# Scan stages of a state-space and feed-forward kernel: the place of the raw copy, the owner of one product, the order of the row and column copies, and the waits of the down projection

## The chip, the cores and the metric

The kernel runs on one core of a Trainium2 chip. The core has TensorE (PE), VectorE (DVE), ScalarE (ACT) and GpSimd (POOL), and a SyncE (SP) queue that issues most of the copies between memory and SBUF. The metric is the device time of one execution in microseconds (us); lower is better.

## The reference, cut to what matters

The input `x` is (4, 1024, 1024) in float32. First a selective state-space layer (Mamba) with `x`'s layer norm as its gate:

```
x  = in_proj_w @ ctx                       # 1024 channels, 1024 time steps, 4 sequences
u  = silu(causal_conv4(x) + conv_b)
x_dbl = x_proj_w @ u                       # rows: 32 of dt, 16 of B, 16 of C
delta = softplus(dt_proj_w @ dt + dt_b)
state[n] = state[n] * exp(delta * A[n]) + delta * u * B[n, t]      # n = 0..15, scan over t
y = sum_n state[n] * C[n, t] + D * u
out = x0 + tanh(g0) * y * silu(layernorm(x0))
```

Then a layer that picks 128 of the 1024 rows of each sequence by a score, runs rotary attention and a gated feed-forward (`silu(h @ w_gate) * (h @ w_up) @ w_down`, width 4096) on the 512 picked rows together, and writes them back into `x` scaled by a gate.

## The kernel before, in words

The four sequences are worked on two at a time. The order of stages is: `project_stage` (input projection, convolution and `x_dbl` for sequences 0 and 1), `scan_stage(0)`, `route_stage(0)` and `layer_stage(0)` (choice, attention), `scan_stage(2)`, `route_stage(2)` and `layer_stage(2)`.

**A scan stage** has `UNITS` = 32 units. A unit is 128 channels (`e` = 0..7) by 512 time steps (one half `th` of a sequence); eight units are a chunk `c`, so that chunks 0 and 2 are the first halves of the two sequences (called even below) and chunks 1 and 3 the second ones (odd). A unit holds 16 states in `NPAIR` = 8 pairs, and every engine walks through slots 0 to 7 of it:

- ACT makes `exp(delta * A)` for both states of pair `i` in slot `i` (L1214), before which `release` (L1103 to L1114) waits until pair `i-2` has left the PSUM banks; beside these it carries the unit's other copies, each tied to a slot by a constant (`READ_AT`, `COPY_AT`, `DU_COPY_AT`, and `RAW_AT`, `PRE_AT`).
- `B * delta * u` comes from POOL for pairs 0, 2, 4, 6 (L733) and from PE for pairs 1, 3, 5, 7 (`make_b`, L862 and L864).
- DVE scans state after state (L1290). The product with C is done by POOL (L757, from the three SBUF buffers `hp`) for the pairs that `pool_pairs` names, and by DVE (L1267, from PSUM) for the others. PE adds the products up (`add_pair`, L882), DVE gates the sum (L1256), POOL adds `x` (L765), SP stores.
- In odd chunks each scan starts from `carry`, saved in the even one.

**The rows of B and C** of a chunk are copied to all 128 partitions by SP: `load_B(c, g)` with 0.5 to 1 MB and `load_C(c, g)` with 1 MB for each group `g` of four states, each after a wait that the chunk before has used the old rows. The B columns (`load_columns`, tile `k_BT`, L129) are eight copies of 2 KB a chunk, double buffered; POOL makes diagonals of them in the chunk's last unit (L747) and ACT scales with them (L1092). SP's list is written out by hand and strictly in order; its first entry of unit `s` is `load_u(s + 2)`, which waits until PE has done `skip(s)` (L869) in slot 3.

**Beside the scans**, `scan_stage(0)` (`early`) projects and convolves sequences 2 and 3: PE runs `late_projection(s)` in slots 1 to 3 of unit `s` and `late_convolution(s - 1)` in slots 5 to 7; ACT's `copy_raw` moves the projection out of PSUM (L1184, L1188, L1191), `copy_pre` the convolution. `scan_stage(2)` (`fill`) runs the feed-forward of the rows picked from sequences 0 and 1 in the gaps of PE: output projection, then `gate_up` in slots from unit 6 to unit 26, then `down` for half of the columns from slot 6 of unit 26. Its weights go through a ring of four tiles that SP fills (L644). POOL's `merge` (L773) multiplies up and gate parts into `hidden`, two of the 32 blocks at a time, and counts `hidden_ready`; `down(m, a)` reads block `m`.

Of the kernel before, what the change touches and what calls it, by code (L numbers as in the profile page):

```python
# [25 lines left out]
NE = DI // P  # L26
NK = DC // P
NS, NR, TAPS = 16, 32, 4
# [3 lines left out]
H2 = L // HALF  # L32
# [4 lines left out]
NI = 4096 // P  # L37
RMS_EPS = 1e-6
SPAN = 2
# [51 lines left out]
class Kept:  # L91
# [22 lines left out]

    def load_delta(self, sp, t, b, sem):
        sp.dma_start(self.dt[:, 0], t["xd"][b * ND:b * ND + NR, 0:HALF]).then_inc(sem, 16)
        self.load_columns(sp, t, b, 0, 0, sem)

    def load_states(self, sp, t, b, g, sem):
        at = b * ND + NR + 4 * g  # L120
# [2 lines left out]
        at += NS  # L123
        sp.dma_start(self.bC[:, 4 * g:4 * g + 4], t["xd"][at:at + 4, 0:HALF].partition_broadcast(P)).then_inc(sem, 16)

    def load_columns(self, sp, t, b, th, j, sem):
        for k in range(NS // 2):
            at = b * ND + NR + 4 * (k // 2) + 2 + k % 2
            sp.dma_start(self.BT[:, j, k], t["xd"][at:at + 1, th * HALF:(th + 1) * HALF].rearrange("n (a p) -> p (n a)", p=P),  # L129
                         allow_slow_non_contiguous=True).then_inc(sem, 16)  # L130
# [238 lines left out]


def pool_pairs(first, s):
    return (1, 3, 5, 6, 7) if s // NE % H2 else (1, 3, 5, 7)


def vec_pairs(first, s):
# [30 lines left out]
FILL_END = DOWN_FROM + DOWN_HALF  # L406
SIZE_LAG, LOG_LAG, SIGMOID_LAG, SWISH_LAG, UP_LAG, MERGE_LAG = 3, 3, 6, 5, 3, 4
WEIGHTS_AT = (0, 2, 5)
RAW_AT, PRE_AT = 0, 3
LATE_PROJECTION = ((), (0, 1), (2,), (3,), (), (), (), ())  # L410
LATE_CONVOLUTION = ((), (), (), (), (), (0,), (1,), (2, 3))

# [1 line left out]
def scan_stage(nc, t, ctx, keep, first, late_taps=None):  # L414
# [93 lines left out]
    def chunk(s):  # L508
        return s // NE
# [42 lines left out]
    with nc.Block() as block:  # L552
        @block.sync
        def _(sp):
# [28 lines left out]
            def load_dt(c):  # L583
                b, th = first + c // H2, c % H2
                if c >= 2:
                    sp.wait_ge(dt_done, NE * (c - 1))
                sp.dma_start(dt[:, c % 2], xd[b * ND:b * ND + NR, th * HALF:(th + 1) * HALF]).then_inc(dt_in[c % 2], 16)
                if c >= 2:
                    sp.wait_ge(xT_ready, NT * NE * (c - 1))
                    if scaled:  # L590
                        sp.wait_ge(diag_ready, ND_B * (c - 1))
                keep.load_columns(sp, t, b, th, c % 2, BT_in[c % 2])

            def load_B(c, g):
                if c >= SPAN * H2:
# [64 lines left out]
                sp.dma_start(ln2[:], t["cols"][:, NH + 2 * NKV + KT:]).then_inc(ln2_in, 16)  # L660
            for s in range(UNITS):
                c, e = chunk(s) + 1, s % NE
                load_u(s + 2)
                load_end(s + 1)
                if e == 0 and s:
                    load_C(c - 1, 2)
                    load_C(c - 1, 3)
                if e == 0 and c < SPAN * H2:
                    load_dt(c)
                if fill:  # L670
                    for k in weights_at(s, 0):
                        load_weights(k)
                if e == NE - 1:
                    load_B(c, 0)
                    load_B(c, 1)
                if fill:
                    for k in weights_at(s, 1):
                        load_weights(k)
                if e == NE - 1:
                    load_B(c, 2)  # L680
                    load_C(c, 0)
                if early and s + 1 < UNITS:
                    load_late(s + 1)
                    if e == 2 and c < SPAN * H2:
                        load_ctx(c)
                if early and s >= 2:
                    store_pre(s - 2)
                if e == NE - 1:
                    load_B(c, 3)
                    load_C(c, 1)  # L690
                if s:
                    store(s - 1)
                if fill and s == (WO_DONE[1] + BASE_LAG) // NPAIR:
                    sp.wait_ge(base_ready, H2 * SPAN)
                    sp.dma_start(t["base0"].rearrange("(a p) c -> p a c", p=P), base).then_inc(base_out, 16)
                if fill:
                    for k in weights_at(s, 2):
                        load_weights(k)
            store(UNITS - 1)
            if early:  # L700
                store_pre(UNITS - 2)
# [117 lines left out]
        def _(pe):  # L819
# [109 lines left out]
            def down(m, a):  # L929
                tile = TILES_UP + m // 2  # L930
                if m % 2 == 0 and a == 0:
                    pe.wait_ge(w_in[tile % RING], 16 * (tile // RING) + 16)
                if m == 0:
                    pe.wait_ge(swish_ready, NI // 2)
                    pe.wait_ge(up_ready, NI // 2)
                    pe.wait_ge(hidden_ready, NI // 2)
                last = nc.tensor.matmul((p_gate, p_up)[a][:], hidden[:, m, a * P:(a + 1) * P],
                                        ring[:, tile % RING, m % 2 * HALF:(m % 2 + 1) * HALF], start=m == 0, stop=m == NI - 1)
                if m % 2 == 1 and a == 1:
                    last.then_inc(w_used, 1)  # L940
# [102 lines left out]
        def _(act):  # L1043
# [162 lines left out]
            for s in range(UNITS):  # L1206
                act.wait_ge(delta_ready, s + 1)
                for i in range(NPAIR):
# [13 lines left out]
                    if s + 1 < UNITS:  # L1222
# [3 lines left out]
                            softplus_exp(s + 1)  # L1226
                        elif i == READ_AT + 2:
                            softplus_ln(s + 1)
                    if early and i == RAW_AT and s:
                        if s == 1:  # L1230
                            act.wait_ge(halo_made, 1)
                        copy_raw(s - 1)
                    if early and i == PRE_AT and s >= 2:
                        copy_pre(s - 2)
                    if i == COPY_AT:
# [5 lines left out]
                    if i > DU_COPY_AT:  # L1241
                        make_states(s + 1, PARTS_AT[i - 1] % PARTS, PARTS_AT[i])
            if early:
                copy_raw(UNITS - 1)
                copy_pre(UNITS - 2)
                copy_pre(UNITS - 1)
            if fill:
# [1149 lines left out]
```

## Time and profile before

| what | value |
|---|---|
| median of 3 runs | 2808.98 us (2807.94 to 2814.0) |
| the profiled execution | 2810.57 us, of which its span 2808.7 us |
| PE, PE weight loads | 2534.9 us (90%), 1853.5 us (66%) |
| DVE | 1964.8 us (70%) |
| ACT, POOL | 1616.4 us (58%), 1616.2 us (58%) |
| first scan of the first stage to the last one's end | 160 to 955 us |
| the same of the second scan stage | 1248 to 2106 us |

Busy shares are means over stages with different limits. A row of the timeline gives start, duration, engine, line, operation, tiles written and read, the count of instructions merged in it, and in brackets how long the engine had stood idle and what it waited for. Durations of neighbours on an engine overlap a little, so the pace is read from start to start.

### The profile page before, as it was taken

What the parts mean: (1) busy time and instruction counts of PE and PEld (TensorE: products, weight loads), DVE (VectorE), ACT (ScalarE), POOL (GpSimd) and SP (SyncE); (2) the same over time, 40 slices, a digit from 0 to 9 for tenths busy, and PEclk for the clock granted to TensorE, in tenths of its full rate; (3) what the DMA queues carried; (4) which work ended last, traced back from release to release, by engine and by line L of the source; (5) the groups of instructions that cost most, each with busy time, mean ns of one, the idle gap of its engine ahead of it and who ended that gap; (6) DMA issues with size and microseconds to landing.
All of it is one profiled execution on the core that took longest, in us unless ns stands there. A gap on an engine that the chain in (4) does not pass through costs nothing. (4 is left out here: it accounts for less than half of the span.)

```text
span 2808.7 us, 38267 instructions
## 1 busy us (share of the span) xinstructions
PE 2534.9 (90%) x13528; PEld 1853.5 (66%) x13528; DVE 1964.8 (70%) x2500; ACT 1616.4 (58%) x3482; POOL 1616.2 (58%) x898
## 2 busy tenths in 40 slices
PE   8979999989999657879999999999997799999998
PEld 3356666666666426556688988888673576578853
DVE  5679999989999786569998988999896544110000
ACT  4578888778887442277787787887661215210000
POOL 1269999999999610028899998889881100000000
PEclk9979999999999858999999999999998899999999
DMA  7732242442332397863344344244228741344442
GB/s 277 260 87 83 64 144 80 127 115 64 116 92 80 110 405 263 291 192 99 121 135 129 103 153 146 84 167 146 85 76 311 273 151 38 97 158 150 152 155 97
DMA packets 252622, 412.53 MB, mean 147 GB/s; under 512 B 50832, under 2 KB 134800, under 8 KB 249872
## 3 DMA queue, kind: packets, MB, share of 16 engines
q1 hardware_dynamic: 238928, 353.98, 39.4%
q10 hardware_dynamic: 12160, 51.39, 4.6%
q0 software_dynamic: 1344, 4.72, 0.5%
q8 instruction: 108, 1.77, 0.3%
q14 instruction: 82, 0.67, 0.1%
HBM read 325.09 MB, written 84.94 MB: 146 GB/s over the span
## 5 line engine op out<-in xcount | busy, mean ns | idle before, releaser
L757 POOL TENSOR_TENSOR s_x<-s_hp,k_bC 128x1024 f32<-128x1024 f32 x288 | 680.2, 2368 | 68.2 <-DVE s_hp L1290 67.7
L733 POOL TENSOR_TENSOR s_x<-s_du,k_bB 128x1024 f32<-128x1024 f32 x254 | 601.5, 2377 | 39.2 <-PE s_py L882 23.6
L882 PE MATMUL s_py<-k_ident,s_x 128*128 128x128 f32 x4096 | 522.2, 274 | 21.4 <-POOL s_x L757 21.4
L882 PEld LDWEIGHTS s_py<-k_ident,s_x 128*128 128x128 f32 x4096 | 463.8, 142 | 32.6 <-POOL s_x L757 28.5
L1214 ACT ACTIVATE s_pA<-s_delta,k_negA 128x512 f32<-128x512 f32 x512 | 333.6, 681 | 190.6 <-DVE s_x L1267 185.1
L1983 PE MATMUL l_p<-l_hT,l_ring 128*128 128x256 f32 x1792 | 389.4, 380 | 2.0 <-ACT l_hT L2088 1.0
L1983 PEld LDWEIGHTS l_p<-l_hT,l_ring 128*128 128x128 f32 x1792 | 341.6, 191 | 49.6 <-issue 1.5
L1290 DVE TENSOR_TENSOR_SCAN s_hp<-s_x,s_carry,s_pA 128x512 f32<-128x512 f32 x256 | 321.7, 1267 | 44.5 <-PE s_pA L864 36.1
L1214 ACT ACTIVATE s_x<-s_delta,k_negA 128x512 f32<-128x512 f32 x512 | 340.6, 710 | 0.0
L1290 DVE TENSOR_TENSOR_SCAN s_hp<-s_x,s_pA 128x512 f32<-128x512 f32 x256 | 310.0, 1211 | 42.3 <-ACT s_x L1214 26.5
L1092 ACT ACTIVATE s_xT<-s_duT,k_BT 128x128 f32<-128x128 f32 x1024 | 336.4, 389 | 0.1
L864 PEld LDWEIGHTS s_pA<-k_bB,s_duT 128*128 128x128 f32 x2048 | 251.0, 196 | 86.2 <-DVE s_hp L1290 68.0
L1290 DVE TENSOR_TENSOR_SCAN s_pA<-s_pA,s_x 128x512 f32<-128x512 f32 x256 | 299.8, 1214 | 4.4 <-ACT s_pA L1214 4.0
L864 PE MATMUL s_pA<-k_bB,s_duT 128*128 128x128 f32 x2048 | 262.8, 283 | 23.0 <-DVE s_hp L1290 23.0
L1267 DVE TENSOR_TENSOR s_x<-s_pA,k_bC 128x1024 f32<-128x1024 f32 x224 | 268.7, 1199 | 17.7 <-DMA k_bC<-scratch_xd 17.7
L1290 DVE TENSOR_TENSOR_SCAN s_pA<-s_pA,s_carry,s_x 128x512 f32<-128x512 f32 x192 | 234.6, 1268 | 1.0 <-ACT s_pA L1214 0.8
L1960 POOL DMA_INDIRECT out_dram<-c_rows,l_row_i x2 | 1.9, 953 | 330.8 <-DVE c_rows L2309 330.8
L862 PEld LDWEIGHTS s_pA<-k_ident,s_xT 128*128 128x128 f32 x1024 | 116.5, 142 | 97.4 <-DVE s_hp L1290 72.1
L862 PE MATMUL s_pA<-k_ident,s_xT 128*128 128x128 f32 x1024 | 135.9, 276 | 39.1 <-DVE s_hp L1290 39.1
L2304 DVE TENSOR_TENSOR t_hidden<-l_silu,l_p 128x256 f32<-128x256 f32 x32 | 13.5, 421 | 208.0 <-PE l_p L1983 208.0
L1990 PE MATMUL l_p<-l_ring,t_hidden 128*128 128x512 f32 x352 | 151.4, 592 | 0.0
L1950 POOL TENSOR_TENSOR l_squares<-l_squares,l_minus_half 128x1 f32<-128x1 f32 x2 | 1.1, 555 | 250.3 <-DVE l_squares L2280 250.3
(238 smaller groups left out, 3770.4 us busy)
## 6 DMA issues: line engine op xcount, KB each, us to landing
k_bC<-scratch_xd SPq DMA_DIRECT2D x32, 1024.0 KB, 11.0
scratch_ug<-p_ug ACTq DMA_DIRECT2D x16, 1024.0 KB, 4.1
k_u<-scratch_ug SPq DMA_DIRECT2D x64, 256.0 KB, 3.5
k_bB<-scratch_xd SPq DMA_DIRECT2D x32, 512.0 KB, 8.3
s_gy<-scratch_ug SPq DMA_DIRECT2D x64, 256.0 KB, 4.5
s_xt<-in_x SPq DMA_DIRECT2D x64, 256.0 KB, 4.8
scratch_x<-s_xt SPq DMA_DIRECT2D x64, 256.0 KB, 3.6
r_x<-scratch_x SPq DMA_DIRECT2D x32, 512.0 KB, 10.2
```

Of the source, the lines that this page charges most:

```text
L733: pool.tensor_tensor(out=x[:, 4 * g:4 * g + n], in0=du[:, s % 2:s % 2 + 1].broadcast_to([P, n, HALF]), in1=bB[:, into:into + n], op=ALU.mu ...
L757: pool.tensor_tensor(out=x[:, 2 * i:2 * i + 2], in0=hp_of(s, i), in1=bC[:, 2 * i:2 * i + 2], op=ALU.mult).then_inc(pool_hc, 1)
L862: last = nc.tensor.transpose(out, xT[:, k, a * P:(a + 1) * P], ident[:])
L864: last = nc.tensor.matmul(out, duT[:, a * P:(a + 1) * P], diagB[:, 2 * scaled.index(i) + n % 2, a], start=True, stop=True)
L882: last = nc.tensor.matmul(py[:, a], x[:, n, a * P:(a + 1) * P], ident[:], is_transpose=True, start=False, stop=n == NS - 1 and a == HALF / ...
L1092: last = nc.scalar.activation(xT[:, k, a * P:(a + 1) * P], duT[:, a * P:(a + 1) * P], ACT.Copy, scale=BT[:, chunk(s) % 2, column(2 * TURNE ...
L1214: nc.scalar.activation(out, delta[:, s % 2], ACT.Exp, scale=negA[:, s % NE, n:n + 1]).then_inc(dA_ready, 1)
L1267: nc.vector.tensor_tensor(x[:, 2 * i:2 * i + 2], pA[:, j:j + 2], bC[:, 2 * i:2 * i + 2], ALU.mult).then_inc(vec_hc, 1)
L1290: nc.vector.tensor_tensor_scan(out, dA, added, initial, ALU.mult, ALU.add).then_inc(scanned, 1)
L1983: last = nc.tensor.matmul(out[:, 0:ROWS], w[:, c * P:(c + 1) * P], src[:, c], start=c == 0, stop=c == KT - 1)
L1990: last = nc.tensor.matmul(banks[2 * a + h][:], src[:, a * P:(a + 1) * P], w[:, h * HALF:(h + 1) * HALF], start=is_first, stop=is_last)
L2304: nc.vector.tensor_tensor(hidden[:, m], silu[:, m % 2], acc[2 + m % 2][:, 0:ROWS], ALU.mult).then_inc(act_ready, 1)
```

## The change

1. `copy_raw(s)` is done in slot 6 of unit `s` and no longer in slot 0 of unit `s + 1`.
2. `pool_pairs` is (1, 3, 5, 7) in every chunk; in odd chunks it was (1, 3, 5, 6, 7). DVE multiplies pair 6 there.
3. `load_C(c, 2)` is asked for at the end of a chunk's last unit and `load_C(c, 3)` as the first entry of the next unit; both stood behind `load_u` and `load_end` of that unit.
4. The eight column copies, in one row in a chunk's first unit, become two at the end of each of its first four units.
5. `down` waits at its first block for all but the last merge, and for the last at block 28.

```diff
-        self.load_columns(sp, t, b, 0, 0, sem)
+        self.load_columns(sp, t, b, 0, 0, range(NS // 2), sem)
...
-    def load_columns(self, sp, t, b, th, j, sem):
-        for k in range(NS // 2):
+    def load_columns(self, sp, t, b, th, j, which, sem):
+        for k in which:
...
 def pool_pairs(first, s):
-    return (1, 3, 5, 6, 7) if s // NE % H2 else (1, 3, 5, 7)
+    return (1, 3, 5, 7)
...
-RAW_AT, PRE_AT = 0, 3
+RAW_AT, PRE_AT = 6, 3
...
                 sp.dma_start(dt[:, c % 2], xd[b * ND:b * ND + NR, th * HALF:(th + 1) * HALF]).then_inc(dt_in[c % 2], 16)
+
+            def load_columns(c, which):
+                b, th = first + c // H2, c % H2
                 if c >= 2:
                     sp.wait_ge(xT_ready, NT * NE * (c - 1))
                     if scaled:
                         sp.wait_ge(diag_ready, ND_B * (c - 1))
-                keep.load_columns(sp, t, b, th, c % 2, BT_in[c % 2])
+                keep.load_columns(sp, t, b, th, c % 2, which, BT_in[c % 2])
...
             for s in range(UNITS):
                 c, e = chunk(s) + 1, s % NE
+                if e == 0 and s:
+                    load_C(c - 1, 3)
                 load_u(s + 2)
                 load_end(s + 1)
-                if e == 0 and s:
-                    load_C(c - 1, 2)
-                    load_C(c - 1, 3)
...
                     for k in weights_at(s, 2):
                         load_weights(k)
+                if e < NS // 4 and c < SPAN * H2:
+                    load_columns(c, (2 * e, 2 * e + 1))
+                if e == NE - 1:
+                    load_C(c, 2)
...
                     pe.wait_ge(up_ready, NI // 2)
+                    pe.wait_ge(hidden_ready, NI // 2 - 2)
+                if m == NI - 4:
                     pe.wait_ge(hidden_ready, NI // 2)
...
-                    if early and i == RAW_AT and s:
-                        if s == 1:
+                    if early and i == RAW_AT:
+                        if s == 0:
                             act.wait_ge(halo_made, 1)
-                        copy_raw(s - 1)
+                        copy_raw(s)
...
             if early:
-                copy_raw(UNITS - 1)
                 copy_pre(UNITS - 2)
```

## Rows read from the trace of the kernel before

**Rows 1.** Timeline of DVE, unit 3 of the first scan stage.

```profile
235.72 2.35 DVE L1290 TENSOR_TENSOR_SCAN s_pA<-s_pA,s_x 128x512 f32<-128x512 f32 x2
239.26 1.22 DVE L1290 TENSOR_TENSOR_SCAN s_hp<-s_x,s_pA 128x512 f32<-128x512 f32 x1 [1.20 <-ACT s_x L1214]
...
256.88 1.20 DVE L1290 TENSOR_TENSOR_SCAN s_hp<-s_x,s_pA 128x512 f32<-128x512 f32 x1
...
260.28 2.34 DVE L1290 TENSOR_TENSOR_SCAN s_pA<-s_pA,s_x 128x512 f32<-128x512 f32 x2
```

**Rows 2.** Timeline of ACT in the same unit.

```profile
236.78 0.58 ACT L1184 ACTIVATE s_raw<-s_p_in 128x512 f32<-128x512 f32 x1
...
237.54 0.97 ACT L1092 ACTIVATE s_xT<-s_duT,k_BT 128x128 f32<-128x128 f32 x3
...
238.51 1.32 ACT L1214 ACTIVATE s_x<-s_delta,k_negA 128x512 f32<-128x512 f32 x2
...
255.65 1.32 ACT L1214 ACTIVATE s_x<-s_delta,k_negA 128x512 f32<-128x512 f32 x2
```

**Rows 3.** Timeline of DVE, unit 13 of the first scan stage (an odd chunk).

```profile
481.25 2.44 DVE L1290 TENSOR_TENSOR_SCAN s_pA<-s_pA,s_carry,s_x 128x512 f32<-128x512 f32 x2
484.79 1.28 DVE L1290 TENSOR_TENSOR_SCAN s_hp<-s_x,s_carry,s_pA 128x512 f32<-128x512 f32 x1 [1.10 <-PE s_pA L864]
...
491.35 0.69 DVE L1256 TENSOR_TENSOR s_gy<-s_py,s_gy 128x512 f32<-128x512 f32 x1 [0.62 <-PE s_py L882]
...
505.97 1.26 DVE L1290 TENSOR_TENSOR_SCAN s_pA<-s_pA,s_carry,s_x 128x512 f32<-128x512 f32 x1
```

**Rows 4.** Window in that chunk: length, busy us of PE, PEld, DVE, ACT, POOL, PE clock, DMA.

```profile
456.00:530.00 74.00, 68.43 (x427) 49.52 (x426) 68.84 (x61) 59.30 (x127) 73.76 (x37) 1.00 0.23 65
```

**Rows 5.** Timeline of DVE, unit 9, the second of that odd chunk.

```profile
385.32 2.44 DVE L1290 TENSOR_TENSOR_SCAN s_pA<-s_pA,s_carry,s_x 128x512 f32<-128x512 f32 x2
...
401.43 1.20 DVE L1267 TENSOR_TENSOR s_x<-s_pA,k_bC 128x1024 f32<-128x1024 f32 x1
402.55 1.27 DVE L1290 TENSOR_TENSOR_SCAN s_hp<-s_x,s_carry,s_pA 128x512 f32<-128x512 f32 x1
...
408.43 1.27 DVE L1290 TENSOR_TENSOR_SCAN s_pA<-s_pA,s_carry,s_x 128x512 f32<-128x512 f32 x1
```

**Rows 6.** Waits of the whole span: us in total, times, longest.

```profile
DVE s_x L1267 <- DMA k_bC<-scratch_xd: 17.7, 6, 3.7
```

**Rows 7.** Groups by line and shape, 160 to 955 us: busy us, mean ns, idle before.

```profile
L1267 DVE TENSOR_TENSOR s_x<-s_pA,k_bC 128x1024 f32<-128x1024 f32 x112 | 134.3, 1199 | 8.1 <-DMA k_bC<-scratch_xd 8.1
```

**Rows 8.** Timeline of DVE, unit 16 of the first scan stage.

```profile
567.83 0.69 DVE L1256 TENSOR_TENSOR s_gy<-s_py,s_gy 128x512 f32<-128x512 f32 x1 [2.01 <-PE s_py L882]
```

**Rows 9.** Timeline of SP's queue, unit 8 of the second scan stage.

```profile
1469.81 1.00 SPq L613 DMA_DIRECT2D k_bC<-scratch_xd  x2
...
1471.55 10.84 SPq L129 DMA_DIRECT2D k_BT<-scratch_xd  x8
1482.43 0.50 SPq L644 DMA_DIRECT2D s_ring<-in_w_up  x1
```

**Rows 10.** Timeline of PE, second scan stage, units 9 and 26.

```profile
1486.83 2.93 PE L924 MATMUL s_p_up<-s_h2T,s_ring 128*128 128x256 f32 x6 [3.09 <-DMA s_ring<-in_w_up]
...
1972.60 1.60 PE L937 MATMUL s_p_gate<-s_ring,t_hidden 128*128 128x512 f32 x2 [4.10 <-POOL t_hidden L773]
```

**Rows 11.** Timeline of ACT, unit 26 (the last copy of an up part).

```profile
1966.56 0.58 ACT L1134 ACTIVATE t_hidden<-s_p_up 128x512 f32<-128x512 f32 x1
```

**Rows 12.** Windows in the second scan stage, columns as in rows 4.

```profile
1484.90:1491.80 6.90, 4.97 (x17) 4.41 (x18) 2.21 (x3) 3.95 (x9) 5.56 (x3) 0.51 0.66 239
1700.00:1703.40 3.40, 3.40 (x17) 3.35 (x16) 3.40 (x4) 3.40 (x10) 3.40 (x2) 0.50 0.43 15
1973.10:1979.90 6.80, 6.80 (x9) 2.21 (x8) 0.51 (x1) 2.41 (x4) 6.26 (x3) 0.50 0.00 0
...
1542.00:1672.00 130.00, 129.83 (x889) 117.00 (x888) 119.56 (x108) 102.70 (x213) 125.09 (x64) 1.00 0.35 115
```

## The prediction

> **What bounds the kernel now.** I read the page first, for which stages each engine is busy in, then only the two scan stages, since nothing else is touched. In them three views answer: windows (who is full), the timeline of each engine over one unit (where DVE stands idle, for DVE carries the scans and sets the pace), and SP's timeline at a chunk's edge. A unit's length is the time between its first scan and the next unit's.
>
> Even units of the first scan stage last 24.56 us (235.72 to 260.28) and hold one idle time of DVE, 1.20 us at pair 1, which waits for ACT's exponential [rows 1]. ACT comes late to it because of the raw copy: from its first instruction to the one behind it ACT spends 237.54 - 236.78 = 0.76 us, and the exponential follows at 238.51 [rows 2]. Thirteen such units look alike, 2 to 7 and 17 to 23.
>
> Odd units there last 24.72 us, and DVE stands idle 1.10 + 0.62 us in each, both times for PE [rows 3], which is itself held up by POOL's products: POOL is busy 73.76 of 74 us [rows 4]. POOL is the bound of odd chunks. What DVE could do is seen in the chunk's second unit, before POOL has fallen behind: 23.11 us (385.32 to 408.43) [rows 5].
>
> At each chunk's edge DVE waits for the C rows of group 2: six waits, 17.7 us in all [rows 6], of which 8.1 in the first scan stage [rows 7], so 9.6 in the second. In unit 16 DVE waits another 2.01 us for the sum of the unit before [rows 8], again POOL's arrears.
>
> The second scan stage is PE's: 129.83 of 130 us busy, though POOL with 125.09 and DVE with 119.56 are close [rows 12]. There PE stands still twice for something this change moves: 3.09 us for a weight tile that SP asked for late, and 4.10 us at the first block of the down projection for POOL's last merge [rows 10]. After each the granted clock is half, 1.2 GHz, for 6.9 and 6.8 us, and once more for 3.4 us just after the edge at unit 16 [rows 12].
>
> **The change part by part.**
>
> *Raw copy to slot 6.* The 0.76 us of ACT leave the front of pair 1. The wait there falls from 1.20 to 1.20 - 0.76 = 0.44 us. They come back ahead of pair 7, whose exponentials began at 255.65 [rows 2]; the first takes half of the merged 1.32, so it ended near 256.34, and DVE took pair 7 up at 256.88 [rows 1]. That is some 0.5 us of cover, so 0.76 - 0.5 = 0.26 us comes out as a new wait. Net 0.76 - 0.26 = 0.5 us a unit, for units 1 to 7, 16 and 17 to 23: 15 x 0.5 = 7.5. Bounds: the whole 0.76 is won (11.4), or the new wait is as long as the old one was (0). The copy needs the projection, which PE ends in slot 3, and late convolution reads it a unit later, so nobody else is made to wait. In odd units DVE isn't waiting for ACT now, and the copy is shorter by the halo's; I take nothing.
>
> *Pair 6 to DVE, first scan stage.* A product costs DVE 402.55 - 401.43 = 1.12 us of its pace [rows 5]. An odd unit at DVE's own pace becomes 23.11 + 1.12 = 24.2; with POOL no longer full I take 24.1, as its wait of some 0.2 at pair 1 shrinks when the raw copy leaves. Units 11 to 15 and 27 to 31, ten of them, gain 24.72 - 24.1 = 0.6 each: 6.0. Two behind each edge lose, since they run at the 23.1 of unit 9 today: 4 x 1.0 = 4.0. Units 8 and 24 take the 1.12 too and get, as I choose, half of it back from a POOL that has less to catch up with: 1.0 lost together. Where an odd chunk ends, unit 16's 2.01 goes [rows 8]. Sum: 6.0 - 4.0 - 1.0 + 2.0 = 3.0. Bounds: nothing at all hidden, 16 x 1.12 = 17.9 lost against those 2.0; or 24.72 comes down to 23.7, which makes 7.
>
> *C rows earlier.* The request of group 2 moves from behind `load_u`, which stands until slot 3, to the end of the unit before, nearly half a unit sooner. DVE's waits are at most 3.7 us long [rows 6] and end with this copy. What is late next would be group 3, which moves forward too, or group 1, asked for where it was. I take all 8.1 in the first stage. In the second PE is the bound, and DVE's wait costs only what PE can't work through; I take two thirds of the 9.6, 6.4. Bounds: 0 if another copy takes its place, and all 9.6 with half of the 3.4 us at half clock, 11.3.
>
> *Columns in pairs.* Eight copies hold SP for 10.84 us, and the weight tile of `w_up` is asked for only behind them, at 1482.43 [rows 9]; PE then waits till 1486.83 [rows 10]. Without them and without the two C requests (1469.81 to 1471.55) the tile is asked for 1482.43 - 1469.81 = 12.6 us earlier and the wait goes: 3.09. At half clock 4.97 us of PE work were done that full clock does in half: 2.5. Together 5.6; bounds 3.09 and 3.09 + 3.45. Two copies at the end of four units stand ahead of `load_u`, which waits anyway; cost nothing, and if that cover were gone up to 10.84 / 4 = 2.7 us of SP a unit.
>
> *Down in two steps.* PE waits 4.10 us for the merge. The other conditions of the first block were met: the last up part was copied by 1966.56 + 0.58 = 1967.14 [rows 11], 5.5 us before PE went on at 1972.60. Block 28 comes five units later (26 entries of PE's list a unit, 4 a block), so the second wait costs nothing. With the clock: 4.10, and PE was busy all of the 6.8 us, so up to half of them, 3.4. PE's idle time was also a chance for DVE and POOL to catch up, so I take a little less than the 7.5, 6.5; bounds 4.1 and 7.5.
>
> *Pair 6 to DVE, second scan stage.* 16 odd units get 1.12 us more of DVE and 2.33 less of POOL. In the window of some five such units DVE is free 130 - 119.56 = 10.4 us, 2.1 a unit, more than the 1.12 [rows 12]. I take 0. Bounds: 16 x 1.12 = 17.9 lost; or 0.3 a unit, 5, won since POOL too was nearly full.
>
> Sum: 7.5 + 3.0 + 8.1 + 6.4 + 5.6 + 6.5 = 37.1. The profiled execution's own time is 2810.57, 1.9 more than its span, so 2773.5; it stood 1.6 above the median of the runs, 2808.98, which gives 2772, the time I predict.
>
> **The rivals.**
>
> *A, PE keeps its time in the second stage.* The C rows and the weights come sooner, but PE meets the next limit at once, or DVE's extra product eats what it gives: 6.4 + 5.6 = 12 lost from the sum, 2784. For it: PE is full there. Against: the half clock and the waits are PE's own.
>
> *B, the wait for C rows only moves.* The request comes sooner, but right behind 0.5 MB and 1 MB copies of the same edge; DVE then waits for group 1 or 2 as long. 8.1 + 6.4 = 14.5 lost, 2786.5. Against: behind the last request of the old unit SP asks for nothing until slot 3, so the engines of the copies have that time.
>
> *C, slower: the product joins the chain.* With pair 6 in PSUM, ACT may not begin the next unit's pair 0 until DVE has multiplied (`release`), and the scan waits for that exponential: product 1.12 and exponential 0.7 us in line, 1.8 a unit in 32 odd units, 58 us, in place of my 3.0: 2772 + 3 + 58 = 2833. It decides from (37.1 - 3.0) / 32 = 1.07 us a unit on, so the product alone, wholly in the open, would make the change even. Against: even units multiply pair 6 in the same way, and no wait stands there, scan 15 covers it (the idle marks of [rows 1] have only pair 1).
> The Trainium skill (Perfetto Trace Analysis, Optimizing Scalar/DVE Operations) says that offloading from a saturated VectorE, even to GpSimd, may make sense, though it might not help, since the two share a read port. By it, taking the product back onto VectorE would be a loss of the kind of C. No run here shows it either way yet; the odd chunks of before show GpSimd, not VectorE, as the full one.
>
> *D, the raw copy costs at its new place.* The whole 0.76 stands before pair 7 in all 32 units, and pair 1's wait, held by PE's `make_b` as well, stays: 7.5 lost and 24.3 added, 2804. Against: the 0.5 us of cover.
>
> **How the numbers follow.** Chances: forecast 0.66, A 0.13, B 0.08, C 0.05, D 0.05, others of both signs 0.03. 0.2% is 5.6 us, about what this measurement can tell from no change. Faster by more: the forecast, A, B, most of D (2804 is just beyond 2803.4, and its milder forms are faster) and a third of the others: 0.91. Slower: C but for its mild forms: 0.04. Same: 0.05. Downward the bounds leave raw 3.9, odd units 4, C rows 4.9, weights 0.9, down 1 and POOL's relief 5, 20 in all, hardly together; I go 14 down, to 2758. Upward the range takes in A and B and a little of an unhidden product: 2790. Outside lies some 0.18.
>
> **What the changed profile would show.** Raw copy: in even units the idle mark at pair 1 near 0.4, a new one near 0.3 at pair 7, length 24.1. Product: POOL's window in odd chunks below 95%, units of 24.1 without the marks of 0.62. C rows: no wait of L1267 for `k_bC`. Columns: two at a time, no PE wait for `in_w_up`, no half clock near unit 9. Down: no idle before its first matmul, full clock around unit 27. I would be wrong if odd units of the second stage grow by half a microsecond or more, or if new waits for copies stand at the edges.

## The result and the profile after

The changed kernel takes 2770.41 us (median of 4 runs, 2768.73 to 2772.9) where the kernel before took 2808.46 beside it: a ratio of 0.9862, with a 95% interval of 0.9845 to 0.9879. Run once more at the end, it gave 0.9855 (0.9838 to 0.9871). I had predicted 2772. The total was right; the terms of the product, of the columns and, in the second stage, of the C rows were not, and the experiments below are mostly about these.

The profiled execution took 2772.9 us, its span 2771.2 against 2808.7. First the page's totals of the changed kernel:

```profile
PE 2531.1 (91%) x13528; PEld 1845.5 (67%) x13528; DVE 2000.9 (72%) x2532; ACT 1619.6 (58%) x3482; POOL 1543.0 (56%) x866
```

POOL has 73 us less work and DVE 36 more, in the main the 32 products of pair 6 (2.37 us each on POOL, 1.20 on DVE). PE's work is the same, and it is the waits that went.

**Even units of the first stage.** Timeline of DVE, unit 3, the changed kernel:

```profile
236.68 2.35 DVE L1297 TENSOR_TENSOR_SCAN s_pA<-s_pA,s_x 128x512 f32<-128x512 f32 x2
239.46 1.22 DVE L1297 TENSOR_TENSOR_SCAN s_hp<-s_x,s_pA 128x512 f32<-128x512 f32 x1 [0.43 <-ACT s_x L1222]
...
257.40 1.22 DVE L1297 TENSOR_TENSOR_SCAN s_hp<-s_x,s_pA 128x512 f32<-128x512 f32 x1 [0.22 <-ACT s_x L1222]
...
260.83 2.35 DVE L1297 TENSOR_TENSOR_SCAN s_pA<-s_pA,s_x 128x512 f32<-128x512 f32 x2
```

Against [rows 1] the idle time at pair 1 has shrunk from 1.20 to 0.43, and a new one of 0.22 stands at pair 7. The unit is 260.83 - 236.68 = 24.15 us long, where it was 24.56. ACT's timeline of the same unit shows where the new wait is from: the raw copy now stands ahead of pair 7's exponentials (the row at 256.66).

```profile
255.28 0.58 ACT L1192 ACTIVATE s_raw<-s_p_in 128x512 f32<-128x512 f32 x1
...
256.66 1.32 ACT L1222 ACTIVATE s_x<-s_delta,k_negA 128x512 f32<-128x512 f32 x2
```

**Odd units of the first stage.** Timeline of DVE, unit 12, the changed kernel:

```profile
453.85 2.44 DVE L1297 TENSOR_TENSOR_SCAN s_pA<-s_pA,s_carry,s_x 128x512 f32<-128x512 f32 x2
456.31 1.28 DVE L1297 TENSOR_TENSOR_SCAN s_hp<-s_x,s_carry,s_pA 128x512 f32<-128x512 f32 x1
...
475.58 1.20 DVE L1274 TENSOR_TENSOR s_x<-s_pA,k_bC 128x1024 f32<-128x1024 f32 x1
...
477.89 2.44 DVE L1297 TENSOR_TENSOR_SCAN s_pA<-s_pA,s_carry,s_x 128x512 f32<-128x512 f32 x2
```

Neither mark of [rows 3] is left. The unit has one product more (the row at 475.58) and is still shorter, 24.04 us where it was 24.72: DVE now goes through it without a pause. The window over three such units (length, busy us of PE, PEld, DVE, ACT, POOL, PE clock, DMA) says the same, with DVE at 72.06 of 72.12 and POOL at 67.24, where [rows 4] had POOL full:

```profile
453.85:525.97 72.12, 68.27 (x427) 48.95 (x426) 72.06 (x65) 59.77 (x127) 67.24 (x33) 1.00 0.23 66
```

**C rows.** Of the 17.7 us of [rows 6] nothing is left. The page's group of DVE's products with C, all 256 of them:

```profile
L1274 DVE TENSOR_TENSOR s_x<-s_pA,k_bC 128x1024 f32<-128x1024 f32 x256 | 306.8, 1199 | 0.0
```

**Columns and the weight tile.** Timeline of SP's queue around the same edge as [rows 9]:

```profile
1437.24 6.18 SPq L616 DMA_DIRECT2D k_bC<-scratch_xd  x2
...
1451.53 1.28 SPq L647 DMA_DIRECT2D s_ring<-in_w_up  x1
...
1459.06 0.93 SPq L129 DMA_DIRECT2D k_BT<-scratch_xd  x2
```

The second stage starts 18.6 us earlier (1229.4, not 1248.0), so the tile asked for at 1482.43 before would be asked for at 1463.8; it is asked for at 1451.53, 12.3 us sooner (predicted 12.6). PE has no wait for it. Windows over that edge, over units 26 and 27, and over the edge at unit 16, all in the second stage, columns as above:

```profile
1438.00:1489.30 51.30, 51.30 (x354) 46.02 (x352) 49.80 (x46) 40.47 (x85) 49.91 (x26) 1.00 0.65 198
...
1913.00:1964.00 51.00, 49.06 (x311) 38.05 (x310) 49.95 (x46) 40.34 (x85) 46.19 (x24) 1.00 0.34 104
...
1640.00:1680.00 40.00, 40.00 (x272) 35.54 (x270) 37.68 (x35) 33.08 (x75) 37.20 (x20) 1.00 0.78 268
```

PE is busy for the whole of the first and the third, and the granted clock is full in all of them; the three stretches at 0.51 and 0.50 of [rows 12] are gone.

**Down projection.** Timelines of PE and of POOL in unit 26, the changed kernel:

```profile
1934.69 1.04 PE L888 MATMUL s_py<-k_ident,s_x 128*128 128x128 f32 x8
1935.56 1.02 PE L945 MATMUL s_p_gate<-s_ring,t_hidden 128*128 128x512 f32 x2
```

```profile
1938.41 1.27 POOL L779 TENSOR_TENSOR t_hidden<-t_hidden,s_swish 128x512 f32<-128x512 f32 x1
```

The first block starts right behind the `add_pair` before it, with no idle time in brackets, 2.9 us before POOL even begins the last merge. In [rows 10] the same matmul had waited 4.10 us.

**Where the time came from, by chunk.** A chunk's length here is the time from its first scan in DVE's timeline to the next chunk's first scan (for the last one: to its last scan's end). In us:

| kernel | chunks 0 to 3, first stage | chunks 0 to 3, second stage | sum |
|---|---|---|---|
| before | 198.3, 197.9, 201.4, 197.1 | 209.0, 215.3, 219.9, 214.1 | 1653.0 |
| after | 195.3, 192.6, 192.8, 192.7 | 208.7, 211.1, 212.6, 205.5 | 1611.4 |

The stages give 21.2 and 20.3 us, 41.6 together, where I had reckoned 18.6 and 18.5. What lies outside of them took 2808.7 - 1653.0 = 1155.7 before and 1159.7 after. Over all fourteen profiles of this study that remainder lies between 1155.7 and 1163.7 with no order that follows the edits, and the profile of before has one of the two lowest values; so I compare the parts by these sums of chunks, and the whole by the medians.

These sums are not free of chance either. Two profiles of the changed kernel differ by 0.1 us. But unit 0 of the second stage took 27.1 us in the changed kernel and 26.4 in "all but down", whose program is the same there. And unit 1 of the first stage took 25.5 us before and 24.6 in "down alone", again the same program there: around its start PE's granted clock was half for 6.8 us in the one and for 3.4 us in the other. A single profile's sum can be off by some 1 to 2 us.

Of the prediction's own signs of being wrong, one is there in part: of the sixteen odd units of the second stage two have grown by more than half a microsecond, unit 15 from 26.10 to 26.78 and unit 25 from 24.73 to 25.71. No new wait for a copy stands at the edges.

### The profile page after: what moved, and what is told of

Its sections match the earlier page's. It is cut to its first block and busy times, and to the rows that moved or that the text cites. A ratio compares the mean times of both kernels' runs of the same rounds, so it can differ in the third digit from the quotient of the medians.

```text
span 2771.2 us, 38280 instructions
## 1 busy us (share of the span) xinstructions
PE 2531.1 (91%) x13528; PEld 1845.5 (67%) x13528; DVE 2000.9 (72%) x2532; ACT 1619.6 (58%) x3482; POOL 1543.0 (56%) x866
## 5 line engine op out<-in xcount | busy, mean ns | idle before, releaser
L763 POOL TENSOR_TENSOR s_x<-s_hp,k_bC 128x1024 f32<-128x1024 f32 x256 | 606.0, 2367 | 108.3 <-DVE s_hp L1297 107.8
L888 PE MATMUL s_py<-k_ident,s_x 128*128 128x128 f32 x4096 | 516.5, 274 | 5.1 <-POOL s_x L763 4.5
L1297 DVE TENSOR_TENSOR_SCAN s_pA<-s_pA,s_carry,s_x 128x512 f32<-128x512 f32 x256 | 313.0, 1268 | 0.4 <-ACT s_pA L1222 0.2
L1274 DVE TENSOR_TENSOR s_x<-s_pA,k_bC 128x1024 f32<-128x1024 f32 x256 | 306.8, 1199 | 0.0
L870 PE MATMUL s_pA<-k_bB,s_duT 128*128 128x128 f32 x2048 | 263.0, 283 | 27.4 <-DVE s_hp L1297 24.6
```

The costliest lines, as they stand in the source:

```text
L763: pool.tensor_tensor(out=x[:, 2 * i:2 * i + 2], in0=hp_of(s, i), in1=bC[:, 2 * i:2 * i + 2], op=ALU.mult).then_inc(pool_hc, 1)
L870: last = nc.tensor.matmul(out, duT[:, a * P:(a + 1) * P], diagB[:, 2 * scaled.index(i) + n % 2, a], start=True, stop=True)
L888: last = nc.tensor.matmul(py[:, a], x[:, n, a * P:(a + 1) * P], ident[:], is_transpose=True, start=False, stop=n == NS - 1 and a == HALF / ...
L1274: nc.vector.tensor_tensor(x[:, 2 * i:2 * i + 2], pA[:, j:j + 2], bC[:, 2 * i:2 * i + 2], ALU.mult).then_inc(vec_hc, 1)
L1297: nc.vector.tensor_tensor_scan(out, dA, added, initial, ALU.mult, ALU.add).then_inc(scanned, 1)
```

## The experiments

Two theories were put ahead of the runs: P, the parts add up as my sum had them, and Q, some only work beside others. Times are medians, ratios are against the kernel before, run beside them, with 95% intervals. That kernel took 2810.07 beside raw, product and C rows alone and all but the product, 2811.39 beside columns and down alone and the two kernels of the last part, and 2811.09 beside the other four.

### One part alone

**Raw copy alone.**

```diff
-RAW_AT, PRE_AT = 0, 3
+RAW_AT, PRE_AT = 6, 3
```

> The kernel before with the raw copy alone moved to slot 6. Theory P (the parts add up, as in the prediction's sum): even units of the first scan stage fall from 24.57 to 24.15 us, with idle marks of 0.43 at pair 1 and 0.22 at pair 7 as in the changed kernel; odd units stay at 24.72, since GpSimd paces them; 15 units x 0.42 = 6 us less than before. Theory Q (the copy costs as much at the new place as it gave at the old): within 2 us of before.

Measured: 2802.91, ratio 0.9976 (0.9964 to 0.9989). Timeline of DVE, unit 3 of this kernel:

```profile
238.86 1.22 DVE L1289 TENSOR_TENSOR_SCAN s_hp<-s_x,s_pA 128x512 f32<-128x512 f32 x1 [0.42 <-ACT s_x L1214]
...
256.80 1.22 DVE L1289 TENSOR_TENSOR_SCAN s_hp<-s_x,s_pA 128x512 f32<-128x512 f32 x1 [0.23 <-ACT s_x L1214]
```

Both marks are those of the changed kernel, so this edit alone makes them. The chunks of the first stage took 196.2, 197.6, 198.4, 196.3: 6.2 us less, 5.1 of it in the even ones. Odd units stay at 24.72. This is theory P's 6 us. The other 1.4 of this run's 7.6 are in the second stage, where nothing was edited: chunk 1 there has 212.3 instead of 215.3, while chunks 2 and 3 have 1.0 and 1.2 more. For chunk 1, PE's timeline and a window right behind show why:

```profile
1480.24 1.56 PE L924 MATMUL s_p_up<-s_h2T,s_ring 128*128 128x256 f32 x6 [2.54 <-DMA s_ring<-in_w_up]
```

```profile
1480.20:1484.00 3.80, 3.76 (x28) 3.60 (x29) 1.83 (x2) 2.61 (x5) 3.80 (x2) 1.00 0.74 273
```

The wait for the weight tile was a little shorter here, 2.54 us and not 3.09 [rows 10], and this time the granted clock did not fall to half behind it, where [rows 12] have 0.51. Unit 9 took 26.48 us instead of 29.36. With nothing edited in this stage, that one wait thus costs up to 3 us more or less, and the sums of chunks of all kernels that still have it carry this error. Chunk 3's 1.2 is of the same kind: behind the wait for the merge the clock was half for 10.2 us here and for 6.8 before.

**Product alone.**

```diff
-    return (1, 3, 5, 6, 7) if s // NE % H2 else (1, 3, 5, 7)
+    return (1, 3, 5, 7)
```

> The kernel before with pair 6 multiplied by VectorE in odd chunks, and nothing else. Theory P: odd units of the first scan stage at 24.1 to 24.3 us, the waits for C rows all still there (six, 17 us), the sum 3 us less than before. Theory Q (GpSimd's arrears were what the edge waits hid in): the two odd chunks of the first stage go from 198 us to about 8 x 24.2 + 2.6 = 196, unit 16 loses 2.0, together 5 to 6 us less. If the product stood in the open: up to 36 us more. Second scan stage unchanged within 2 us by both.

Measured: 2815.34, ratio 1.0019 (1.0009 to 1.0028). A small loss, where P had 3 us of gain and Q 5 to 6: both failed. Timeline of DVE, one odd unit of this kernel, from 460.81 to 485.42:

```profile
460.81 2.44 DVE L1290 TENSOR_TENSOR_SCAN s_pA<-s_pA,s_carry,s_x 128x512 f32<-128x512 f32 x2
463.84 1.28 DVE L1290 TENSOR_TENSOR_SCAN s_hp<-s_x,s_carry,s_pA 128x512 f32<-128x512 f32 x1 [0.59 <-ACT s_x L1214]
...
485.42 2.44 DVE L1290 TENSOR_TENSOR_SCAN s_pA<-s_pA,s_carry,s_x 128x512 f32<-128x512 f32 x2
```

The waits for PE are gone, as predicted, and another has come in their place: 0.59 us for ACT at pair 1, the wait that even units had. The unit takes 24.61 us instead of 24.72. Only with the raw copy gone as well does it come down to 24.04. So the raw copy is worth 24.61 - 24.04 = 0.57 us in each odd unit too, as soon as POOL no longer hides it. The waits for the C rows are still there, and not smaller:

```profile
DVE s_x L1267 <- DMA k_bC<-scratch_xd: 19.2, 6, 3.6
```

**C rows alone.**

```diff
+                if e == 0 and s:
+                    load_C(c - 1, 3)
                 load_u(s + 2)
                 load_end(s + 1)
-                if e == 0 and s:
-                    load_C(c - 1, 2)
-                    load_C(c - 1, 3)
...
+                if e == NE - 1:
+                    load_C(c, 2)
```

> The kernel before with the C rows of groups 2 and 3 asked for earlier, and nothing else. Theory P: all six waits gone and 8.1 + 6.4 = 14.5 us less than before. Theory Q: an odd chunk of the first stage takes GpSimd 8 x 24.72 = 198 us whether VectorE waits in it or not, and it took 197.9 with the wait, so the waits of units 8 and 24 (5.5 us) give nothing there; only unit 16's 2.5 counts, and in the second stage 5 to 7 us: 8 to 9 us less than before.

Measured: 2789.31, ratio 0.9924 (0.9905 to 0.9943), more than either theory's term. By chunks it is 0.0, 0.2, 4.2, 2.7 in the first stage and 0.1, 6.7, 4.6, 1.9 in the second. Chunk 1 of the first stage gains next to nothing, as Q had it: POOL sets its pace, and what DVE no longer waits for at the edge comes back as a wait for PE later in the chunk. Chunk 3, for which Q had said the same, keeps 2.7; its last unit has no diagonals to make for a next chunk, but that this is the reason is not shown. The first stage gains 7.1 of the 8.1 that P had. Timeline of DVE, unit 15 of the first stage:

```profile
553.67 2.45 DVE L1291 TENSOR_TENSOR_SCAN s_hp<-s_x,s_carry,s_pA 128x512 f32<-128x512 f32 x2 [2.63 <-PE s_pA L863]
```

The 6.7 in the second stage is the surprise. SP's timeline and the window over that edge, this kernel:

```profile
1448.35 6.20 SPq L613 DMA_DIRECT2D k_bC<-scratch_xd  x2
...
1463.52 7.19 SPq L129 DMA_DIRECT2D k_BT<-scratch_xd  x8
1470.75 0.50 SPq L644 DMA_DIRECT2D s_ring<-in_w_up  x1
```

```profile
1462.00:1490.00 28.00, 28.00 (x191) 25.08 (x190) 26.29 (x24) 22.67 (x47) 27.84 (x16) 1.00 0.50 128
```

The eight column copies are still in one row, but without the two C requests right ahead they are issued sooner, and they hold SP 7.19 us instead of the 10.84 of [rows 9]. The weight tile comes in time: PE is busy 28 of 28 us at full clock. This part alone removes the wait that I had given to the columns.

**Columns alone.**

```diff
+                if e < NS // 4 and c < SPAN * H2:
+                    load_columns(c, (2 * e, 2 * e + 1))
```

> The kernel before with the column copies in pairs over four units, and nothing else. Theory P: the wait of TensorE for the weight tile of w_up in unit 9 of the second scan stage (3.09 us) and the half clock behind it go: 5.6 us less than before. Theory Q (the two requests for C rows, still ahead of the weights, are what fills the copy engines): the tile lands late all the same, part of the wait stays, 0 to 3 us less.

Measured: 2804.26, ratio 0.9976 (0.9967 to 0.9985); by chunks 5.2 us, 4.1 of it in chunk 1 of the second stage. SP's timeline of this kernel:

```profile
1470.53 1.00 SPq L616 DMA_DIRECT2D k_bC<-scratch_xd  x2
1472.14 0.53 SPq L647 DMA_DIRECT2D s_ring<-in_w_up  x1
...
1478.52 3.54 SPq L129 DMA_DIRECT2D k_BT<-scratch_xd  x2
```

The tile is asked for at 1472.14 and no longer at 1482.43, 10.3 us earlier though this run's stage starts 1.2 us later, with the C requests where they were. PE doesn't wait for it (unit 9 takes 24.73 us where it took 29.36), as P had it. Either part, the C rows or the columns, is enough to remove PE's wait.

**Down alone.**

```diff
                     pe.wait_ge(up_ready, NI // 2)
+                    pe.wait_ge(hidden_ready, NI // 2 - 2)
+                if m == NI - 4:
                     pe.wait_ge(hidden_ready, NI // 2)
```

> The kernel before with the down projection's two-step wait, and nothing else. Theory P: unit 27 of the second scan stage falls from 31.5 to 24 or 25 us, full clock there, 6.5 to 7.5 us less than before. Theory Q (GpSimd and VectorE, behind in an odd chunk, are the next limit at once): 3 us or less.

Measured: 2804.12, ratio 0.9978 (0.9968 to 0.9987). Chunk 3 of the second stage goes from 214.1 to 206.9, and unit 27 alone from 31.54 to 23.99 us, 7.5: the wait of 4.10 and the whole of the 3.4 us that half clock had cost, with nothing given back: P. The rest of this run's 8.5 by chunks lies in chunks that the edit doesn't touch.

### One part left out

**All but the product.** The changed kernel with this undone:

```diff
-    return (1, 3, 5, 7)
+    return (1, 3, 5, 6, 7) if s // NE % H2 else (1, 3, 5, 7)
```

> The changed kernel with pair 6 back on GpSimd in odd chunks. Theory P: 3 us more than the changed kernel, 34 us less than before. Theory Q: odd chunks of the first scan stage stay at GpSimd's 198 us against 192.7 in the changed kernel, and unit 16 waits 2 us for the sum again: 12 to 13 us more than the changed kernel, so 25 us less than before.

Measured: 2776.96, ratio 0.9882 (0.9864 to 0.9900). By chunks the product is worth 7.0 us here, between P's 3 and Q's 12: 8.1 gained in the first stage (0.8, 3.0, 3.3, 1.0), and 1.1 lost in the second. The 0.8 is in an even chunk, where the product is the same in both kernels; it is the chance of unit 1 told above. In the second stage the units behind two edges, 8 and 24, grow by 1.1 each and units 12 to 15 by 0.35 on average, while unit 16, where POOL's arrears used to come due, shrinks from 29.38 to 26.40. The same edit that loses alone gains when the other four are in place.

**All but the C rows.** The changed kernel with `load_C(c - 1, 2)` and `load_C(c - 1, 3)` back behind `load_end`:

```diff
-                if e == NE - 1:
-                    load_C(c, 2)
+                if e == 0 and s:
+                    load_C(c - 1, 2)
+                    load_C(c - 1, 3)
```

> The changed kernel with the C rows of groups 2 and 3 asked for at their old place. Theory P: the six waits are back, 14.5 us more than the changed kernel. Theory Q (GpSimd no longer paces the odd chunks, so nothing hides a wait of VectorE in them, and a VectorE that arrives earlier waits longer, as with the product alone): six waits of 3 to 3.5 us, 8 to 9 us in the first stage and as much in the second, 18 us more than the changed kernel.

Measured: 2788.77, ratio 0.9919 (0.9903 to 0.9936). The waits of this kernel:

```profile
DVE s_x L1273 <- DMA k_bC<-scratch_xd: 18.2, 6, 3.7
```

18.2 us of waiting cost 2.8 to 4.0 us at each of six edges, 18.8 in all by chunks: 8.9 in the first stage and 9.9 in the second. That is theory Q's 18. Here chunk 1 of the first stage pays 2.9, where the rows alone had gained it 0.2: with POOL relieved, a stop of DVE is no longer caught up. The stretch at half clock at unit 16 of the second stage [rows 12] is back too:

```profile
1689.70:1693.10 3.40, 3.40 (x16) 3.21 (x15) 3.40 (x4) 3.40 (x10) 3.40 (x2) 0.50 1.03 384
```

Every kernel with the C rows at their old place has such a stretch of 3.4 us in unit 16 or 17, and none of those with the new place has one.

**All but the columns.** The changed kernel with this undone:

```diff
-                if e < NS // 4 and c < SPAN * H2:
-                    load_columns(c, (2 * e, 2 * e + 1))
```

and all eight asked for in one row as before.

> The changed kernel with all eight column copies again in the first unit of a chunk. Theory P: 5.6 us more than the changed kernel. Theory Q (the column copies were slow and the weight late only with the two C row copies in front of them, and these stand elsewhere now): the eight take SP 7 us, the weights come 4 us earlier than they did before, TensorE waits for none: the same as the changed kernel within 1 us.

Measured: 2772.22, ratio 0.9857 (0.9833 to 0.9880), not to be told from the changed kernel's 0.9855. By chunks it is 0.3 us: 1.0 more in chunk 1 of the second stage, where the edge is, and 0.65 less in chunk 0, of which all lies in unit 0. Q holds, but for a small wait that is left. Timelines of SP and of PE at the edge, this kernel:

```profile
1449.58 7.86 SPq L129 DMA_DIRECT2D k_BT<-scratch_xd  x8
1457.48 0.50 SPq L644 DMA_DIRECT2D s_ring<-in_w_up  x1
```

```profile
1461.97 1.56 PE L925 MATMUL s_p_up<-s_h2T,s_ring 128*128 128x256 f32 x6 [0.75 <-DMA s_ring<-in_w_up]
```

Of the wait of 3.09 us in [rows 10], 0.75 is left when the eight copies stay together. Beside the C rows the columns' new places hardly matter.

**All but down.** The changed kernel with the old single wait:

```diff
-                    pe.wait_ge(hidden_ready, NI // 2 - 2)
-                if m == NI - 4:
                     pe.wait_ge(hidden_ready, NI // 2)
```

> The changed kernel with the old single wait of the down projection. Theory P: the wait of 4 us and the half clock behind it are back, 6.5 to 7.5 us more than the changed kernel. Theory Q (with pair 6 off GpSimd the last merge comes earlier by up to 2.3 us): a wait of some 2 us and full clock, 2 to 4 us more.

Measured: 2780.19, ratio 0.9890 (0.9873 to 0.9908). PE's timeline, and two windows around its end:

```profile
1940.30 2.05 PE L943 MATMUL s_p_gate<-s_ring,t_hidden 128*128 128x512 f32 x2 [4.09 <-POOL t_hidden L779]
```

```profile
1938.00:1948.00 10.00, 7.71 (x9) 2.66 (x10) 4.36 (x4) 5.32 (x11) 6.76 (x4) 0.60 0.01 2
1940.00:1950.20 10.20, 9.90 (x20) 4.86 (x20) 2.66 (x4) 4.23 (x9) 4.76 (x3) 0.50 0.01 2
```

The wait is back at 4.09, as long as before though POOL has less to do, and with it the fallen clock: a mean of 0.60 over the first window, which takes in the last 2.3 us of the wait, and half over the second. So Q's shorter wait with full clock is out. Unit 27 has 33.1 us where the changed kernel has 24.30, 8.8 more; the sums of chunks differ by 8.1, since unit 0 was 0.7 shorter here. It is more than the 7.2 between before and after in the same unit (31.54 and 24.30), where the clock was half for 6.8 us and not for 10.2.

**The changed kernel again**, beside these three; nothing in it is edited.

> The changed kernel itself, on the same chip and beside the same runs of the kernel before, to stand next to the three that each leave a part of it out: 38 us less than before.

Measured: 2770.77, ratio 0.9855 (0.9838 to 0.9871).

### One step further

Two marks were left in even units, 0.43 at pair 1 and 0.22 at pair 7. **The raw copy one slot later** takes it out from in front of pair 7's exponentials:

```diff
-RAW_AT, PRE_AT = 6, 3
+RAW_AT, PRE_AT = 7, 3
```

> The changed kernel with the raw copy in slot 7 in place of 6, behind pair 7's exponentials, where ScalarE stood idle 0.85 us. Theory P: the mark of 0.22 us at pair 7 goes from the even units and nothing comes for it: 24.15 to 23.93, 16 units, 3.5 us less than the changed kernel. Theory Q: the copy then pushes the exponentials of the next unit's pair 0 or its state copies, and the wait at pair 1 grows by as much: no change.

Measured: 2765.14, ratio 0.9839 (0.9825 to 0.9852), by chunks 5.8 us less than the changed kernel where P had 3.5. Timeline of DVE, unit 3: the mark at pair 7 is gone, that at pair 1 stands, and the unit (234.47 to 258.27) takes 23.80 us. That is 0.35 less than 24.15, more than the mark of 0.22; what the other 0.13 are is not shown.

```profile
237.25 1.22 DVE L1297 TENSOR_TENSOR_SCAN s_hp<-s_x,s_pA 128x512 f32<-128x512 f32 x1 [0.43 <-ACT s_x L1222]
```

**And the scaling of u one slot later.** In the changed kernel ACT scales `u` (0.71 us) between the exponentials of pairs 0 and 1. On top of the last edit:

```diff
-                    if i == 0:
+                    if i == 1:
                         scale_u(s)
```

> As the one before, and the scaling of u moved from slot 0 to slot 1 in both scan stages, behind pair 1's exponentials. Theory P: ScalarE's 0.6 us leave the front of pair 1 too, the mark of 0.43 goes, even units of the first stage at 23.5 us: 16 x 0.65 = 10 us less than the changed kernel. Theory Q: TensorE's make_b for pair 1, which ends about when VectorE is free, sets pair 1: the mark stays at 0.1 to 0.3. In the second stage TensorE needs the scaled u in slot 3; it is there in time by both, no change there.

Measured: 2752.52, ratio 0.9789 (0.9775 to 0.9802), 18 us below the changed kernel where P had 10. Timeline of DVE, unit 3, and windows over three even and three odd units:

```profile
234.37 2.35 DVE L1297 TENSOR_TENSOR_SCAN s_pA<-s_pA,s_x 128x512 f32<-128x512 f32 x2
236.62 1.20 DVE L1297 TENSOR_TENSOR_SCAN s_hp<-s_x,s_pA 128x512 f32<-128x512 f32 x1
...
257.62 2.35 DVE L1297 TENSOR_TENSOR_SCAN s_pA<-s_pA,s_x 128x512 f32<-128x512 f32 x2
```

```profile
234.37:304.12 69.75, 67.62 (x427) 48.95 (x426) 69.47 (x65) 63.50 (x154) 67.11 (x33) 1.00 0.25 69
446.27:517.98 71.71, 68.28 (x427) 48.96 (x426) 71.71 (x65) 59.77 (x127) 67.26 (x33) 1.00 0.24 67
```

No mark is left, and the unit takes 23.25 us, odd ones 23.90. DVE is busy 69.47 of 69.75 and 71.71 of 71.71 us: it is the bound of both kinds of unit in the first stage now, and a further gain there has to take work off it. PE and POOL stand close behind, with 67 to 68 us. P had counted only the even units' pair 1; the odd units gave 0.14 each as well, and the second stage, where neither theory had a change, 1.7.

## Why the prediction was right, and where its terms were not

Gains in us by the sums of chunks (in brackets by the medians):

| part | predicted | alone | left out of the changed kernel |
|---|---|---|---|
| raw copy | 7.5 | 7.6 (7.2), of which 6.2 in the stage that it touches | not run |
| product | 3.0 and 0 | -3.2 (-5.3) | 7.0 |
| C rows | 8.1 and 6.4 | 20.4 (20.8) | 18.8 (18.0) |
| columns | 5.6 | 5.2 (7.1) | 0.3 (1.5) |
| down | 6.5 | 8.5 (7.3) | 8.1 (9.4) |
| sum | 37.1 | 38.5 (37.1) | |
| together | | 41.6 (38.1 and 40.3) | |

The parts alone add up to within a few microseconds of the whole. P thus holds for the total, but not part by part: two couplings of opposite sign lie beneath it. The four parts without the product add up to 41.7 alone, by chunks, and give 34.5 together (all but the product): 7.2 less, 5.7 of it in the second stage, where the wait for the weight tile can be gained only once. The product then gives 7.0 where alone it had lost 3.2: 10.2 more.

- **Raw copy: right in mechanism and size for even units.** Predicted a mark of 0.44, a new one of 0.26 and a unit of 24.1; found 0.43, 0.22 and 24.15. A unit gained 0.42 and not 0.5, and alone the copy gave 6.2 us in the first stage, 5.1 of it in even chunks, not 7.5; that the run's total came to 7.6 is chance in the second stage. The sentence "In odd units DVE isn't waiting for ACT now ... I take nothing" failed: true of the kernel before, and no longer of one in which POOL is relieved.
- **Product: the relief is real, but the term was booked to the wrong edit.** Odd units came out at 24.04 against 24.1, POOL at 67.24 of 72.12 (93%) against "below 95%". Yet the product alone reaches only 24.61; the 0.57 beyond is the raw copy's. My own sentence that the wait at pair 1 shrinks when the raw copy leaves held that condition, and put it at 0.2. Alone, units 8 to 10 and 24 to 26 grow by 1.0 to 1.6 each behind the edges, more than the relief returns, and the sum is a loss. How much of its turn to a gain is due to the raw copy and how much to the C rows is shown only for those 0.57. Unit 16's wait of 2.01 went, as said. In the second stage the 0 was a loss of 1.1 that had two sides: units behind an edge and the end of chunk 1 grew, unit 16 shrank by 3.0, and the long units in PE's full stretch kept their length (unit 10 has 27.5 us with and without the product).
- **C rows: right in the first stage, too small in the second.** 8.1 predicted, 7.1 found alone and 8.9 with the rest in place. In the second stage "two thirds of the 9.6, 6.4" failed: left out of the changed kernel the rows cost 9.9, all of the wait and not two thirds. The stretch at half clock at unit 16, which the prediction had only in its bounds, belongs to them too. Alone they give 13.3 there, since they also bring the weight tile.
- **Columns: the step that failed as an addition.** "Without them and without the two C requests ... the wait goes" named two causes, and the sum then gave the whole of it to one part. Either alone removes the wait, so together they give it once: 5.6 was counted on top of rows that already have most of it. What the columns add beside the rows is 1.0 at that edge (0.3 in the sums).
- **Down: mechanism right, size low.** The first block waits for nothing. I had taken 1.0 off for the idle time lent to DVE and POOL; unit 27 gave the full 7.5 alone, so nothing was lent, and left out it cost 8.8 there, 8.1 in the sums.

The errors cancelled for the most part: by the last column product, rows and down were 4.0, 4.3 and 1.6 too small, and the columns 5.3 too large, while the whole was 41.6 - 37.1 = 4.5 too small. (The last column need not add up to the whole, and the raw copy is missing in it.) A right total thus rested partly on luck, and the total itself showed nothing of it.

**The rivals.** A (PE keeps its time) is out: the second stage gave 20.3, with PE full in the window over the first edge. B (the wait only moves) is out: no product with C waits for anything. C (the product joins the chain) is out at its size: no odd unit of the changed kernel grew by 1.8 us (the most is 0.98, unit 25 of the second stage). Its sign held for the product alone, by other means. The Trainium skill (Perfetto Trace Analysis, Optimizing GPSIMD Operations) advises to prefer other engines over GpSimd where possible, since it is generally slower. The groups agree on the speed (1199 ns a product on DVE, 2367 ns on GpSimd), but followed alone here the advice costs 0.19%, and within the changed kernel it gains. On the shared read port that the prediction names no run here shows anything. D (the raw copy costs at its new place) is out: 0.22 us at pair 7 and no more. The slot 7 kernel took that little away.

What stays open: what the raw copy is worth when left out of the changed kernel, which was not run (the 0.57 us of each odd unit are read from the product alone), how much of the columns' 5.2 alone is the clock's chance at the weight tile, and what the product is worth with only one of raw copy and C rows in place.

## What to carry to other kernels

When two edits remove what stands ahead of the same late instruction, price the wait once and see which edit alone would do; when an edit relieves the engine that sets the pace, go again through everything that this engine had hidden, since its price is no longer nothing. A single part measured alone can have the wrong sign for the set it belongs to (1.0019 for the product), so test a part both ways, alone and left out. And look at what stands between the two exponentials that the scan waits for: moving one more instruction, the scaling of 0.71 us, by a slot gave 11.8 us by chunks, more than either the columns or the down projection.

## What the runs showed of the hardware

- The time for which the same eight 2 KB column copies held SP's queue depended on what went ahead: 10.84 us right behind two requests of 1 MB [rows 9], 7.19 and 7.86 with these asked for earlier; at the next edge where they are asked for, unit 16, 9.82 before and 4.78 and 4.59 in the same two kernels. Two of them took 0.93 us in one place and 3.54 in another, 7 us behind the same requests of 1 MB. So a row of small requests has no fixed price here; what sets it is not shown.
- In all six kernels that have PE's wait of 4.1 to 4.6 us for the merge, the granted clock fell to half around its end, for 6.8 us in four and for 10.2 in two (raw alone and all but down); it stayed full in all of the window where the wait was gone. Taking the wait away was worth 7.2 to 8.8 us in unit 27, about twice its length.
- Around the shorter wait for the weight tile no length of the wait decided it: half clock for 6.8 us with 3.09 us of waiting (before), for 3.4 with 3.19 (down alone) and with 2.37 (product alone), none with 2.54 (raw alone) or 0.75 (all but the columns).
